# Routing a mixture-of-experts layer inside the attention pipeline instead of in a stage of its own

## The reference

```python
x = x + attention(layernorm(x))                 # 16 heads of 16
x = x + mixture(layernorm(x))
def mixture(x):                                 # 8 experts, top 2, F = 352
    probs = softmax(x @ router_weight)          # 256 x 8
    keep the two largest per token (ties: the lower expert)
    y1, y2 = split(x @ w1[e]); o = (silu(y1) * y2) @ w2[e]
    return sum over the two kept experts of probs[e] * o[e]
```

## Time and profile before

| | us |
|---|---|
| median of 3 executions (lowest, highest) | 2424.82 (2421.76, 2430.6) |
| the profiled execution, its own time | 2427.32 |
| its span | 2425.5 |
| busy over the span: TensorE, VectorE, GpSimd, ScalarE | 81%, 71%, 60%, 50% |
| mean granted TensorE clock | 0.897 |

### The profile page before, as it was taken

How to read it: one execution, slowest core, us unless ns; L and a number is a source line. 1 busy time by engine, 2 the same in 40 slices (tenths; PEclk the granted TensorE clock), 3 DMA queues, 4 the chain that set the end, 5 groups by cost and what they waited for, 6 DMA issues and landing times. The chain is left out here.

```text
span 2425.5 us, 33097 instructions
## 1 busy us (share of the span) xinstructions
PE 1973.4 (81%) x10054; PEld 1174.3 (48%) x10054; DVE 1711.0 (71%) x2416; ACT 1220.4 (50%) x2476; POOL 1445.0 (60%) x1146
## 2 busy tenths in 40 slices
PE   2699999998745699955788898989898987649998
PEld 1334444443345699953344343534343433337776
DVE  4587777676156355532799999999999999846554
ACT  1176666666454233323666757576757564322222
POOL 7344444332136344431799999999999999734444
PEclk9699999999855799986899999999898999868999
DMA  3554444431164344430412222222213130011100
GB/s 87 111 108 99 102 104 90 100 84 51 36 187 153 87 76 77 77 56 29 148 65 93 79 79 80 78 88 70 99 59 109 40 121 28 0 63 36 35 26 26
DMA packets 235169, 190.05 MB, mean 78 GB/s; under 512 B 148585, under 2 KB 205553, under 8 KB 235010
## 3 DMA queue, kind: packets, MB, share of 16 engines
q1 hardware_dynamic: 221714, 170.31, 25.2%
q0 software_dynamic: 13296, 17.77, 4.0%
HBM read 138.53 MB, written 49.49 MB: 78 GB/s over the span
## 5 line engine op out<-in xcount | busy, mean ns | idle before, releaser
L1476 POOL TENSOR_TENSOR mb_dbu<-mb_dtu,mb_bbc 128x1024 f32<-128x1024 f32 x256 | 601.4, 2360 | 72.5 <-DVE mb_hp L1618 47.5
L318 DVE TENSOR_REDUCE at_mx<-at_s_ps 128x2 f32<-128x1024 f32 x256 | 312.4, 1223 | 115.8 <-PE at_s_ps L395 115.5
L250 ACT ACTIVATE at_probs<-at_t_ps 128x512 f32<-128x512 f32 x512 | 292.1, 596 | 200.0 <-PE at_t_ps L386 194.2
L1681 PE MATMUL mb_y_ps<-mb_hc,mb_ident 128*128 128x512 f32 x640 | 329.7, 641 | 74.7 <-DVE mb_hc L1626 74.7
L1620 DVE TENSOR_TENSOR_SCAN mb_da_ps<-mb_da_ps,mb_dbu 128x1024 f32<-128x1024 f32 x160 | 365.3, 2283 | 17.2 <-ACT mb_da_ps L1529 17.2
L386 PE MATMUL at_t_ps<-at_qst,at_kst 64*128 64x512 f32 x512 | 203.1, 488 | 47.1 <-ACT at_probs L250 42.0
L1681 PEld LDWEIGHTS mb_y_ps<-mb_hc,mb_ident 128*128 128x128 f32 x640 | 124.0, 203 | 242.4 <-issue 124.2
L1482 POOL TENSOR_TENSOR mb_hp<-mb_hp,mb_cbc 128x1024 f32<-128x1024 f32 x96 | 226.6, 2360 | 0.0
L1618 DVE TENSOR_TENSOR_SCAN mb_hp<-mb_da_ps,mb_dbu 128x1024 f32<-128x1024 f32 x96 | 218.8, 2279 | 0.0
L922 POOL DMA_INDIRECT x<-m_o,m_xs x71 | 110.9, 1562 | 166.9 <-DMA x<-m_o,m_xs 107.3
L1626 DVE TENSOR_TENSOR mb_hc<-mb_da_ps,mb_cbc 128x1024 f32<-128x1024 f32 x160 | 196.0, 1225 | 18.7 <-PE mb_y_ps L1681 1.5
(11 more groups left out here) (282 smaller groups left out, 4420.2 us busy)
## 6 DMA issues: line engine op xcount, KB each, us to landing
mb_bbc<-mb_scr SPq DMA_DIRECT2D x64, 512.0 KB, 6.1
mb_cbc<-mb_scr SPq DMA_DIRECT2D x64, 512.0 KB, 4.9
at_qst<-at_scr SPq DMA_DIRECT2D x192, 64.0 KB, 2.4
at_kst<-at_scr SPq DMA_DIRECT2D x192, 64.0 KB, 2.3
m_xs<-m_xs_list SPq DMA_DIRECT2D x71, 129.0 KB, 2.1
at_scr<-at_qk_hi SPq DMA_DIRECT2D x32, 256.0 KB
at_scr<-at_qk_lo SPq DMA_DIRECT2D x32, 256.0 KB
m_x<-x SPq DMA_DIRECT2D x16, 512.0 KB, 4.4
```

What stands on the lines that cost most here:

```text
L250: act.activation(probs[:, c, h, :], t_ps[:, k % 2, :], ACT.Exp, scale=SCALE).then_inc(exp_done, 1)
L318: dve.tensor_reduce(out, s_ps[:, m % 2, :, :], AX.X, ALU.max).then_inc(max_done, 1)
L1476: pool.tensor_tensor(dbu[:, q % 3, :, :], dtu_2, bbc[:, 2 * p:2 * p + 2, :], ALU.mult).then_inc(S["dbu_ready"], 1)
L1681: last = pe.matmul(y_ps[:, v % 2, :], ident[:, :], src[:, j, :], start=(q == tile_first[v] and j == 0), stop=(q == tile_last[v] and j == 1))
```

## The change

The steps of the routing keep their arithmetic and get slots of the attention pipeline, as distances ("lags") behind the first tile of the batch: `batch(t, lag)` is n in slot t = 4n + lag. The normalised rows come from `xo` in SBUF, not from a second load of `x1`. The transposes, the logits and the counts use `f_ps` and its `f_free`, four transposes at a time. The pipeline has nine more slots, to t = 46. The tables are built behind the loop of VectorE; they have three more rows, for the order in which experts are met. The weights are no longer loaded with the routing: in the expert block, slot t loads and splits the weights of the expert that comes t+2nd, ahead of the tile's other work on SyncE, ScalarE and VectorE, and tile q below 8 waits for the q-th.

| lag | added in slot 4n + lag |
|---|---|
| 6 to 9 | VectorE: statistics of a tile of `xo`, behind `max_pair` 1 |
| 9 | VectorE: aggregates; ScalarE: logarithm, exponential (k = 13, 14) |
| 10 | VectorE: Newton step (`newton`, behind `max_pair` 0); ScalarE: normalised rows (k = 4, 7, 10, 13) |
| 11, 12 | TensorE: four transposes at k = 2; VectorE: copy out (`leave_bank`, behind `max_pair` 1) |
| 13 | TensorE: logits at k = 2; VectorE: maximum, difference; ScalarE: exponential; VectorE: normalise |
| 14 | VectorE: `choose` twice; TensorE: counts at k = 13; VectorE: `rank_rows` behind `max_pair` 6 |
| 15 to 18 | VectorE: positions; ScalarE: copy of the payload; GpSimd: two scatters a slot |

TensorE in the attention phase:

```diff
+                        if k == 13 and (n := batch(t, 14)) is not None:
+                            for free in f_free:
+                                pe.wait_ge(*free)
+                            ranks(n)
+                            f_free = ((R["r_run"], n + 1),)
+                        if k == 2:
+                            stays = [(batch(t, lag), lag) for lag in (11, 12, 13) if batch(t, lag) is not None]
+                            for n, lag in stays:
+                                for free in f_free:
+                                    pe.wait_ge(*free)
...
+                                if lag < 13:
+                                    rows_T(n, lag - 11)
+                                    f_free = ((R["r_T"], 2 * n + lag - 10),)
+                                else:
+                                    logits(n)
+                                    f_free = ((R["r_z"], n + 1),)
                         if k in (4, 8, 11, 15):
                             for free in f_free:
                                 pe.wait_ge(*free)
```

VectorE in the attention phase:

```diff
                     max_pair(ahead, 0)
...
+                    if (n := batch(t, 10)) is not None:
+                        newton(n)
+                    if (n := batch(t, 14)) is not None:
+                        choose(n, 0)
...
                     max_pair(ahead, 1)
+                    leave_bank(t)
...
                     max_pair(ahead, 2)
...
+                    if (n := batch(t, 14)) is not None:
+                        choose(n, 1)
+                    if (n := batch(t, 15)) is not None:
+                        places(n)
```

SyncE loads nine small constants in slot -4 and waits for `r_norm` of batch n-1 before it reloads `xo`. The expert block, on SyncE, ScalarE, VectorE and TensorE:

```diff
+        def weights(t):
+
+            return t + 2 if 0 <= t + 2 < E else None
...
+                    if (s := weights(t)) is not None:
+                        e = sp.value_load(route.expert_at[0:1, s:s + 1], min_val=0, max_val=E - 1)
+                        for j in range(3):
+                            if s:
+                                sp.wait_ge(S["lo_done"], 3 * s - 2 + j)
+                            for dst, src, _, _ in pieces(s, j, e):
+                                sp.dma_start(dst, src).then_inc(w_in[j], 16)
...
+                    if (s := weights(t)) is not None:
+                        for j in range(3):
+                            act.wait_ge(w_in[j], (32 if j == 2 else 16) * (s + 1))
+                            for src, _, dst, _ in pieces(s, j):
+                                last = act.activation(dst, src, ACT.Copy)
+                            last.then_inc(S["hi_done"], 1)
...
+                    if (s := weights(t)) is not None:
+                        for j in range(3):
+                            dve.wait_ge(S["hi_done"], 3 * s + j + 1)
+                            for src, _, part, dst in pieces(s, j):
+                                last = dve.tensor_tensor(dst, src, part, ALU.subtract)
+                            last.then_inc(S["lo_done"], 1)
...
+                        if q < E:
+                            pe.wait_ge(S["lo_done"], 3 * q + 3)
```

More of the change, by code:

```diff
@@ L234, in _ @@
                         chain(pool.tensor_tensor(y, y, a, ALU.mult), 5 * u + 5)
-                    if t % 4 == 3 and tile(t) is not None:
-                        n = t // 4
+                    if (n := batch(t, 5)) is not None:
                         pool.wait_ge(xo_loaded, 16 * (n + 1))
@@ L239, in _ @@
                         pool.tensor_tensor(xo[:, n % 2, :, :], xo[:, n % 2, :, :], bo_all, ALU.add).then_inc(xo_biased, 1)
+                    if t == 0:
+                        prepare_rows()
+                    for j in range(4):
+                        if (n := batch(t, 15 + j)) is not None:
+                            scatter(n, j // 2, (2 * (j % 2), 2 * (j % 2) + 1))
+                for c in range(2):
+                    for n in (NB - 2, NB - 1):
+                        landed(pool, c, n)
             @block.scalar
@@ new lines, in leave_bank @@
+                def leave_bank(t):
+                    for h in range(2):
+                        if (n := batch(t, 11 + h)) is not None:
+                            dve.wait_ge(R["r_T_ps"], 2 * n + h + 1)
+                            wait(dve, R["r_logits"], n)
+                            dve.tensor_copy(rT[:, :, 2 * P * h:2 * P * h + 2 * P], f_ps[:, :].rearrange("p (k c) -> p k c", k=2)).then_inc(R["r_T"], 1)
+                    if (n := batch(t, 13)) is not None:
+                        z_in = f_ps[:, 0:4 * E0].rearrange("p (k e) -> p k e", k=4)
+                        dve.wait_ge(R["r_logits"], n + 1)
+                        steps(dve.tensor_reduce(zmax[:, :], z_in, AX.X, ALU.max))
+                        dve.tensor_tensor(pr[:, :, :], z_in, per_row(zmax[:, :]), ALU.subtract).then_inc(R["r_z"], 1)
@@ L338, in _ @@
                     max_pair(ahead, 2)
+                    if (n := batch(t, 9)) is not None:
+                        dve.wait_ge(R["r_stats"], 4 * n + 4)
+                        wait(dve, R["r_norm_set"], n)
+                        for a in range(4):
+                            last = dve.bn_aggr(rmv[:, a, :], rstats[:, a, :])
+                        last.then_inc(R["r_var"], 1)
+                    if (n := batch(t, 14)) is not None:
+                        choose(n, 1)
+                    if (n := batch(t, 15)) is not None:
+                        places(n)
                     if (u := tile(t - 1)) is not None:
@@ new lines, in _ @@
+                steps(dve.tensor_tensor(past, per_tile(slot_no[:, :]), per_expert(ends[:, :]), ALU.is_ge))
+                steps(dve.tensor_tensor(part, past, per_expert(gap[:, :]), ALU.mult))
+                steps(dve.tensor_reduce(table[:, :], part, AX.X, ALU.add))
+                steps(dve.scalar_tensor_tensor(table[:, :], slot_no[:, :], float(P), table[:, :], ALU.mult, ALU.add))
+                steps.mark(dve.tensor_scalar(route.first_row[:, :], table[:, :], float(LIST), None, ALU.min))
@@ new lines, in _ @@
+                steps.mark(dve.tensor_tensor(late, per_tile(slot_no[:, 0:E0], E0), per_expert(rising[:, :], E0), ALU.is_ge))
+                steps(dve.tensor_tensor(part, past, per_expert(used[:, :]), ALU.mult))
+                steps.mark(dve.tensor_reduce(near[:, :], late, AX.X, ALU.add))
+                steps(dve.tensor_reduce(table[:, :], part, AX.X, ALU.add))
+                steps.mark(dve.tensor_scalar(route.expert_at[:, :], near[:, :], float(E0 - 1), None, ALU.min))
+                steps.mark(dve.tensor_scalar(route.place[:, :], table[:, :], float(E0 - 1), None, ALU.min))
@@ L969, in look_up @@
                 def look_up(q):
[L970 removed]
+                    index[q] = pe.value_load(route.place[0:1, q:q + 1], min_val=0, max_val=E - 1)
                 look_up(0)
+                pe.wait_ge(S["const_in"], 16)
                 for t in SLOTS:
```

555 lines of the change are left out of this document (244 added, 311 removed).

## The result

The changed kernel takes 2476.97 us (median of 4 runs, 2470.77 to 2477.91) beside 2427.71 us of the kernel before (4 runs): a ratio of 1.020, 95% interval 1.017 to 1.023. It is slower by some 49 us; 2429 was forecast, and 2458 was the upper end of the range. The profiled execution took 2477.91 us, its span is 2476.1.

A forecast was written before the change was run, and what follows sets the result against it. TensorE was taken to bound full slots and expert block, a chain the routing. 58 us lost in full slots, minus 82.7 saved in the tail, plus 29 lost in the expert block: +4, so 2429 us; range 2394 to 2458.

The forecast's parts named there:

- What bounds it: TensorE sets the full slots' time, busy 457 of 493 us; its work at an unlucky point is paid in full.
- Part 1: Full slots: TensorE's added transposes, logits and counts cost 3.9 us a batch, 20 us for five batches.
- the nine constants: SyncE's loads of about 0.37 us each, hidden in the fill; at most 4 us if nothing hides them.
- Part 2: Full slots: waits for the shared bank and late VectorE, 11.8 us a batch; 58 us lost, added instructions included.
- The prediction's own sign of it: Full slots: the forecast is wrong if the granted clock leaves 1.00 before slot 30.
- The clock rival: Full slots: new stalls lower TensorE's clock in five or six slots, another 27 us, 2456 us; chance 0.15.
- Absorbed waits: Full slots: stalls let ScalarE catch up, so these slots cost only 25 us, time 2396 us; chance 0.20.
- Part 3: Tail, slot 32 to the expert block's first load: 78.6 us in place of 161.3, 82.7 saved, bounds 72 and 90.
- Part 4: Expert block: weights through one buffer, about 6.1 us a cycle, delay the first tiles; 29 us lost, bounds 22 and 42.
- The rival of a cycle of 8 us: Expert block: weights slowed by loads sharing the DMA engines, 14 us more, 2443 us; chance 0.10.

The follow-up runs named there:

- the kernel with the filled wait: The changed kernel plus eight useless 512-column matmuls ahead of the k = 4 wait in slots of lags 11, 12 and 13: 2451.61 us, ratio 1.0105.
- the two doses: The kernel before plus, at k = 2, eight 8-column products in five slots and eight 512-column products in five others, without waits: 2458.43 us, ratio 1.013.
- the copy-first kernel: The changed kernel with one line moved, so VectorE empties f_ps ahead of max_pair 1 instead of behind it: 2425.41 us, ratio 0.999.
- the kernel with the stall alone: The kernel before plus a VectorE copy that TensorE awaits at k = 4 in 15 slots, nothing of the routing: 2460.85 us, ratio 1.013.
- kernel with the products apart: The copy-first kernel with lag 13's eight logit products placed one by one between TensorE's other matmuls: 2443.93 us, ratio 1.005.

## Why the prediction was wrong

**What bounds it** was right: in the full slots TensorE's time is the slot's time, and what it gets at an unlucky point is paid in full.

**Part 1** (instructions) held: transposes 0.66 us for 0.5, logits 1.95 for 1.8. That the nine constants sit hidden in the fill did not: they hold up SyncE's queue and slot 6 is 3.2 us late, near the 4 us given as the bound.

**Part 2 is the step that failed.** Its waits were right: 1.91 us of stall for 2.0, 1.64 for 1.7, both released by the instruction that was named. At the full clock its slots of lags 11 and 12 were nearly right as well: 19.8 forecast, 19.4 in the kernel with the filled wait. What failed is the step behind it, which priced each wait at its own length (2.0 of stall and 0.5 of transposes, "2.5 us a slot") and left what the wait does to TensorE's clock out of the sum: the term was 58 us and measured 107.7 at slot 32. The prediction's own sign of it, the granted clock leaving 1.00 before slot 30, came at t = 11. Adding up (1 - granted clock) x length over slots 11 to 31 gives 72 us; 7 of them are slot 31's, whose clock was as low before (0.65). So up to 65 us of the growth is clock (an upper estimate, since idle time in it costs nothing), and the rest, about 40, stands where 58 were forecast. The step failed on both sides: where the clock held, 1.7 us of idle time cost only 1.0 to 1.3, and where it fell, 2.3 to 2.6. Two triggers of the clock are shown: the stalls of lags 11 and 12, by removing and by filling them, and the block of 8-column products (lag 13), by the two doses, which the prediction saw only as 1.8 us of instructions. What the stall of lag 13 adds to that block does not show: the clock of slot 13 was 0.85 with the stall, 0.84 without it and 0.85 with it filled. What brings the clock down in lag 14, where a wait of 0.7 us and ten narrow products (the counts) stand together, was not separated; it fell there in three of five slots of the copy-first kernel as well.

**The clock rival** had this mechanism and was given 0.15, with "five or six" falls of 5 us each, 27 us. It was 18 slots (slot 31 left out) of 3.6 us on average, by the estimate above. The evidence set against it was one stall: 2.33 us idle at 650 us that left the clock at 1.00. Such a single case decides nothing. That very stall, 2.33 us in slot 33, brought the clock down in two other executions: in the kernel with the stall alone the projection behind it took 2.79 us and the slot had 0.81, in the kernel with the two doses 3.44 us and 0.72. And the stall alone brought it down 9 times and left it 6 times. With some twenty new waits in 20 slots the question was not whether one can pass, but how many would, and that asked for about half the chance and a range up to 2480. The Trainium skill, TensorE: Matmul & The Clock Gate, "A second HAM failure mode: psum-queue depth-cycling", says that micro-idle gaps between groups of matmuls make the clock alternate; this case's traces agree with it in the slots of lags 11 and 12: nine of ten below 1.00 with the gap, and nine of ten at 1.00 without it.

**Absorbed waits** did not happen: no slot with transposes at 18.5 us or below except where the bank was emptied first.

**Part 3** was right: 79.7 us for 78.6. The part that it did not see is that 15 us of the 161.3 belonged to the weights and not to the chain of batches.

**Part 4** was right within its bounds: 24.5 us for 29, tile 0 at 14.3 for 16.3, tile 6 at 47.7 for 53, a cycle of 5.1 to 6.2 us for 6.1. The rival of a cycle of 8 us is out.

## What to carry to other kernels

When a change puts a wait into a stretch that TensorE bounds, price its length and put at least as much again into the range for the clock behind it (here up to 65 us beside 40), unless work stands in the gap; and price a run of narrow products as a gap too. Before a bank is shared in such a stretch, look at what stands ahead of the instruction that empties it on its engine: here one line's order was worth 51 us. Matmuls that share the array stay in one piece.

## What the runs showed of the hardware

- A block of 16 matmul instructions of 8 columns in 1.95 to 2.48 us brought TensorE from 2.4 to 1.2 GHz in five of five slots though the engine counted as busy, and in 23 of 25 over five kernels; 1.9 us of products of 512 columns in none of five.
- The same idle time of 1.70 us at the same place of a slot brought the clock down in 9 of 15 slots. The same instructions can meet either level: slot 31, unchanged in both, took 19.8 us at 0.65 in the kernel before and 14.9 us at 1.00 in the kernel with the two doses:

```profile
658.80:673.70 14.90, 11.88 (x60) 4.46 (x64) 1.15 (x3) 10.36 (x19) 3.61 (x2) 1.00 0.00 0
```

- The kernel with the products apart spread over 17 us between executions. That the clock's falls differ between them is likely, but not shown: each kernel has one profile.
- Value products of 32 columns each: four heads in 1.06 us back to back, 1.04 us for each head when a product with a 128x128 stationary operand stood between them. The Trainium skill, TensorE: Matmul & The Clock Gate, "Part 3: Packing small matmuls", says that tiles of the array run concurrently; the traces agree, and show what breaks it.
